# Two graph layers on one core: seven-product sets begun two columns earlier with their sums made in place, and block row 0 worked off in four stripes

## The chip, the cores and the metric

The kernel runs on one core of one Trainium2 chip. The metric is the device time in microseconds (us) of a whole execution; lower is better.

## The reference

Two residual graph layers over 8192 nodes with 64 features, all in float32. `adj` is a dense 8192 x 8192 array of 256 MiB that is used by both layers.

```python
def layer0(x, adj, u):                 # dropout on x, then the graph product
    keep = (u >= 0.1)
    return adj @ (x * keep / 0.9)
def layer1(x, adj, weight, bias):
    return adj @ (x @ weight) + bias
x = layernorm(x + layer0(x, adj, u))   # call it h
x = layernorm(x + layer1(x, adj, weight, bias))
```

## The kernel before

The adjacency is cut into 16 x 16 tiles of 512 x 512 numbers (1 MiB each), `adj_t[i, j]`, laid out on the host as [128, 4, 512]: four slices of 128 sources j by 512 outputs i. `stat` holds for each block j the dropped-out x (64 numbers) and, once it is known, h (64 numbers); they are the stationary operands, a tile is the moving one. TensorE writes 64 result rows at a time, so that products go in couples: one into the lower 64 PSUM partitions, one into the upper 64, side by side. One matmul of the program is two records of the trace.

Row i of h needs all 16 tiles of row i with x (layer 0). Column j of the second product needs h of block j. A tile (i, j) with j < i can serve both on one visit. A tile with j > i comes too early for h; it is kept on the chip when it is within HOLD = 3 of the diagonal, else loaded a second time (78 tiles, so 334 loads in all).

The function `order_of_work` writes out one list of jobs, which all engines follow:

- **first** (i, j): the tile with x, four matmuls of 512 columns (L731) into the two banks `sum_f`.
- **second** (L806) and **pair** (L800): one or two tiles with h into one of three `echo` banks; VectorE then adds the bank to `layer2` (`join`, L554 and L644).
- **both**: first and second on one tile. **early** (L784): two tiles of columns 0 to 3, rows 4 to 15, with x and with h in turn, two echo banks, added to `layer1` and `layer2`.
- **fused**, in rows above EARLY = 4 and columns 4 to 13: seven products on quarters of the tile instead of eight, 14 matmuls of 256 columns (L749 to L766). Four of its seven operand pairs are sums of quarters, which VectorE makes in `operands` (L581, L583, L584) in a buffer apart, `tile_sums`, up to AHEAD = 3 jobs ahead. The products of a row gather in two `products` banks; `combine` adds them up once per row.
- **row_end**, **turn**: ScalarE and VectorE copy the row's sum to `halves` (L447, L651, L655), TensorE transposes it (L824), VectorE and ScalarE make the layernorm (L668 to L676), and h of the block is ready. FILL = 6 half jobs stand after row_end to cover this chain.
- **final** (L839): the product with the weight, eight times at the end, then the second layernorm and the store.

The planner keeps a running `lead`: each job adds its TensorE time (WORK) and takes off 16 for each load; with the lead under LEAD it takes a heavy or early job, else a light one. In the inner loop at most MOST_IN_A_ROW = 2 heavy jobs follow each other while others are left. `place_tiles` gives each tile one of SLOTS = 16 slots of 8 KiB per partition; SyncE issues all loads in order (L392), each behind the tile job that frees its slot. x and u come in five groups through the last four slots (L370, L371), and VectorE drops out and reduces them (L528 to L544); the maximum of |x| gives the scale of h.

VectorE is in order: it walks the same list, doing the joins, the sums for fused jobs, the combine and the layernorm chain.

Of the kernel before, what the change touches and what calls it, by code (L numbers as in the profile page):

```python
# [30 lines left out]
P = 128  # L31
# [9 lines left out]
SLOTS = 16  # L41
EARLY = 4
HOMES = 5
AHEAD = 3
# [3 lines left out]
WORK = {"first": 11, "second": 11, "both": 22, "fused": 19, "pair": 22, "early": 44}  # L48
# [6 lines left out]
XU_GROUPS = ((4, 5), (5, 8), (8, 12), (12, 16), (0, 4))  # L55
XU_BEFORE = (1, 3, 6, 10)
# [18 lines left out]
TILE_JOBS = ("fused", "both", "first", "second", "pair", "early")  # L75
HALVES = {"first": 1, "second": 1, "both": 2, "fused": 2, "pair": 2, "early": 4}


def tiles_of(job):
    kind, i, j = job  # L80
    return [(i, j), (i + 1, j)] if kind in ("pair", "early") else [(i, j)]

# [14 lines left out]

def order_of_work():
# [6 lines left out]
    def put(job):  # L105
        nonlocal lead
        if job[0] in ("first", "both", "fused", "early"):
# [6 lines left out]
    for i in range(NB):  # L114
# [5 lines left out]
        if i >= 1:  # L120
            filler = []
            while sum(HALVES[job[0]] for job in filler) < FILL:
                choice = [early] if lead < LEAD and early else [again] if i > 7 else []
                choice = [jobs_of for jobs_of in (*choice, light, again, early, heavy, near) if jobs_of]
                filler.append(choice[0].pop(0))
                put(filler[-1])
                if len(filler) == 1:
                    jobs.append(("turn", i - 1))
            for job in seconds_of([r for r in range(NB) if held(r, i - 1)], i - 1):
                put(job)  # L130
            again += seconds_of([r for r in range(i - 1) if not held(r, i - 1)], i - 1)
            if i - 1 < EARLY:
                early = sorted(early + [("early", r, i - 1) for r in range(EARLY, NB, 2)], key=lambda job: job[1:])
# [40 lines left out]
    return jobs  # L174


def place_tiles(jobs):
# [7 lines left out]
    for m, job in enumerate(tile_jobs):  # L185
        for tile in tiles_of(job):
            if tile not in on_chip:
                on_chip[tile] = len(needs)
                needs.append([tile, m, []])
            needs[on_chip[tile]][2].append(m)  # L190
            if not (job[0] == "first" and held(*tile)):
                del on_chip[tile]

    free = [(0, s, 0) for s in range(SLOTS)]
    loads, place = [], {}
    for tile, begin, uses in needs:
        free.sort(key=lambda t: t[0])
        freed, slot, use = free.pop(0)
        assert freed <= begin, "the order of work needs more slots"
        loads.append((*tile, slot, use, freed, tile_jobs[begin][0]))  # L200
        free.append((uses[-1] + 1, slot, use + 1))
        for m in uses:
            place[tile_jobs[m], tile] = (slot, use)
# [3 lines left out]
def resnorm_graph_layers(nc: bass.Bass, x, adj_t, u, weight, bias, out):  # L207
# [15 lines left out]
    latest_freed, freed_for = 0, {}  # L223
    for load in loads:
        latest_freed = max(latest_freed, load[4])
        freed_for[load[0:2], load[5]] = latest_freed


    sums_from, chain_at = [], 0
    for job in jobs:  # L230
        if job[0] in ("row_end", "turn"):
            chain_at = done_after[job]
        elif job[0] == "fused":
            n = len(sums_from)
            begin = max(tile_jobs.index(job) - AHEAD, freed_for[job[1:3], "fused"], chain_at)
            if n >= 2:
                begin = max(begin, tile_jobs.index(fused_jobs[n - 2]) + 1)
            sums_from.append(begin)
    joined = [job for job in jobs for _ in range({"second": 1, "both": 1, "pair": 1, "early": 2}.get(job[0], 0))]
    finals = [job[1] for job in jobs if job[0] == "final"]  # L240

    complete = {i: max(n for n, job in enumerate(joined) if job[1] in (i, i + 1)) + 1 for i in range(0, NB, 2)}
# [7 lines left out]
    with ctx:  # L250
# [10 lines left out]
        tile_sums = sb("tile_sums", [P, 2, 4, 2, B // 2])  # L261
# [26 lines left out]
        def stat_sums(j):  # L288


            n = j - EARLY
            home = stat_homes[:, n] if n < HOMES else layer1[:, n - HOMES]
            return home.rearrange("p (v k f) -> p v k f", v=4, k=2)

# [31 lines left out]

        s_arrived = [sem(f"tile_arrived_{n}") for n in range(SLOTS)]
        s_xu = [sem(f"xu_loaded_{n}") for n in range(len(XU_GROUPS))]
# [8 lines left out]
        half_by_dve = sem("half_of_row_summed")  # L337
        operands_ready = sem("tile_sums_ready")
# [21 lines left out]

        row_0 = [job[2] for job in jobs if job[0] in TILE_JOBS][:NB]
        assert row_0 == sorted(row_0, key=lambda j: [a <= j < b for a, b in XU_GROUPS].index(True))

# [3 lines left out]
        def _(sp):  # L367
# [7 lines left out]
            for n, (i, j, slot, use, freed, kind) in enumerate(loads):  # L375
# [7 lines left out]
                if i == rows_begun and kind in ("first", "fused"):  # L383
                    if i >= 2:
                        sp.wait_ge(turned_read, i - 1)
                    sp.dma_start(x_res[:, i % 2], x_v[:, i]).then_inc(s_res[i % 2], 16)
                    rows_begun += 1
                if use == 0 and staged <= slot:
# [3 lines left out]
                sp.dma_start(tiles[:, slot], adj_t[i, j]).then_inc(s_arrived[slot], 16)  # L392
# [6 lines left out]
        def _(pool):  # L399
# [9 lines left out]
            pool.wait_ge(turned_read, NB)  # L409
            pool.wait_ge(turned_ready, NB)  # L410
            pool.wait_ge(h_ready, NB)
# [17 lines left out]
        def _(act):  # L429
# [10 lines left out]
            for job in jobs:  # L440
                if job[0] == "row_end":
                    i = job[1]
                    if i:
                        act.wait_ge(turned_ready, i)
# [3 lines left out]
                elif job[0] == "turn":  # L448
                    act.wait_ge(centred, job[1] + 1)
# [8 lines left out]
        def _(dve):  # L458
# [59 lines left out]
            def pair_inverse_root(n):  # L518
                if n >= 2:
                    dve.wait_ge(y_ready, n - 1)  # L520
                return inverse_root(rstd[:, n % 2], var[:, n % 2], root[:, n % 2], 2 * C, NB + n + 1)
# [35 lines left out]
            n_operands = 0  # L557
            n_combined = 0

            def sum_stat(j):  # L560

                dve.wait_ge(h_ready, j + 1)
# [10 lines left out]
            def operands(n):  # L573

                _, i, j = fused_jobs[n]
                if n >= 2:
                    dve.wait_ge(tile_jobs_done, done_after[fused_jobs[n - 2]])
                slot, use = place[fused_jobs[n], (i, j)]
                dve.wait_ge(s_arrived[slot], 16 * (use + 1))
                tile, a = tiles[:, slot], tile_sums[:, n % 2]  # L580
                step(dve.tensor_tensor(out=a[:, 0:2], in0=tile[:, 0:2].rearrange("p k (v m) -> p v k m", v=2),  # L581
                                       in1=tile[:, :, B // 2:B].rearrange("p (v k) m -> p v k m", v=2), op=ALU.add))
                step(dve.tensor_tensor(out=a[:, 2], in0=a[:, 1], in1=tile[:, 0:2, 0:B // 2], op=ALU.add))  # L583
                dve.tensor_tensor(out=a[:, 3], in0=tile[:, 2:4, 0:B // 2], in1=a[:, 2],  # L584
                                  op=ALU.add).then_inc(operands_ready, 1)

            def combine(i):
# [18 lines left out]
                step(plus(second[:, left], products[1][high, right]), 3)  # L606
# [261 lines left out]
```

## Time and profile before

| | us |
|---|---|
| median of 3 runs | 920.83 (919.95 to 921.16) |
| profiled execution, own time | 920.42 |
| profiled execution, span | 918.6 |
| TensorE matmul busy | 884.0 |
| VectorE busy | 448.6 |
| ScalarE, GpSimd busy | 28.7, 24.3 |
| DMA | 359.49 MB, mean 391 GB/s |

The span is what the profiler recorded from the first to the last instruction; 1.8 us of the execution's time lie outside it. "Busy" of TensorE counts the time in which at least one matmul is under way. A mean duration of a matmul includes its way through the array, so that two neighbours overlap; the pace is read from the starts.

### The profile page before, as it was taken

To read this page: it belongs to the slowest core of one execution; us is meant where nothing else is said; L and a number is where in the kernel's file an instruction comes from. 1 tells how busy PE (TensorE), PEld (TensorE's weight loads), DVE (VectorE), ACT (ScalarE), POOL (GpSimd) and SP (SyncE) were. 2 spreads that over 40 slices of the span, in tenths; PEclk is the share of its full clock that TensorE was granted. 3 is DMA by queue.
4 is the path that set the end of the run, shared out by engine and by line. 5 is a ranking of instruction groups with operands and counts; after the bars stand their busy time and mean duration, and the time that the engine had idled before them with its cause. 6 is when DMAs were issued, how large, how long until landed. Compare 5 with 4: busy or idle time off the path is not lost.

```text
span 918.6 us, 11872 instructions
## 1 busy us (share of the span) xinstructions
PE 884.0 (96%) x5070; PEld 363.0 (40%) x5070; DVE 448.6 (49%) x804; ACT 28.7 (3%) x66; POOL 24.3 (3%) x24
## 2 busy tenths in 40 slices
PE   4689999999999999999999999999999999999996
PEld 0123333333333333333444445354544635546342
DVE  4320122114113126155674767586768576777556
ACT  0010000000000000000000000000000000000011
POOL 3000000000000000000000000000000000000123
PEclk9899999999999999999999999999999999999998
DMA  9999999988997989999999999999999999999972
GB/s 350 400 421 421 421 420 422 421 360 352 422 375 281 422 330 376 421 420 416 417 376 420 421 410 418 383 425 383 414 385 411 420 420 421 420 421 420 421 327 69
DMA packets 57348, 359.49 MB, mean 391 GB/s; under 512 B 6352, under 2 KB 14544, under 8 KB 14544
## 3 DMA queue, kind: packets, MB, share of 16 engines
q1 hardware_dynamic: 57296, 358.74, 95.2%
q8 instruction: 40, 0.66, 0.3%
q14 instruction: 12, 0.10, 0.0%
HBM read 356.61 MB, written 2.10 MB: 390 GB/s over the span
## 4 chain that ended last, share of the span: by engine, by line
PE 91%; DMA 5%; SPq 3%; DVE 1%; issue 0%; ACT 0%; DVEq 0%
PE psum L731 23%; PE psum L800 22%; PE psum L784 18%; PE psum L749 6%; PE psum L759 6%; PE psum L764 6%; PE psum L806 5%; DMA tiles<-adj_t 5%; PE psum L754 3%; SPq L392 2%; PE psum L824 1%; PE psum L839 1%; SPq L371 1%; SPq L370 0%; PE psum L766 0%
## 5 line engine op out<-in xcount | busy, mean ns | idle before, releaser
L731 PE MATMUL psum<-tiles,stat 128*64 128x512 f32 x1144 | 263.8, 605 | 25.6 <-DMA tiles<-adj_t 25.5
L554 DVE TENSOR_TENSOR layer<-psum,layer 128x512 f32<-128x512 f32 (+1 forms) x132 | 91.0, 689 | 253.8 <-PE psum L784 160.7
L800 PE MATMUL psum<-tiles,stat 128*64 128x512 f32 x944 | 210.6, 594 | 0.0
L784 PE MATMUL psum<-tiles,stat 128*64 128x512 f32 x768 | 169.1, 593 | 0.4 <-issue 0.4
L731 PEld LDWEIGHTS psum<-tiles,stat 128*64 128x64 f32 x1144 | 81.5, 139 | 189.2 <-issue 143.9
L800 PEld LDWEIGHTS psum<-tiles,stat 128*64 128x64 f32 x944 | 66.5, 137 | 126.3 <-issue 124.9
L581 DVE TENSOR_TENSOR tile_sums<-tiles 128x1024 f32<-128x1024 f32 x65 | 79.5, 1223 | 42.5 <-PE psum L766 39.7
L784 PEld LDWEIGHTS psum<-tiles,stat 128*64 128x64 f32 x768 | 55.2, 137 | 108.3 <-issue 108.3
L751 PE MATMUL psum<-tiles,stat 128*64 128x256 f32 x260 | 66.7, 379 | 0.0
L749 PE MATMUL psum<-tiles,stat 128*64 128x256 f32 x260 | 66.7, 379 | 0.0
L766 PE MATMUL psum<-tile_sums,stat 128*64 128x256 f32 x260 | 66.7, 379 | 0.0
L749 PEld LDWEIGHTS psum<-tiles,stat 128*64 128x64 f32 x260 | 35.6, 137 | 29.0 <-issue 13.7
L806 PE MATMUL psum<-tiles,stat 128*64 128x512 f32 x200 | 47.0, 592 | 0.0
L764 PE MATMUL psum<-tiles,stat_homes 128*64 128x256 f32 x180 | 46.2, 379 | 0.0
L761 PE MATMUL psum<-tile_sums,stat_homes 128*64 128x256 f32 x180 | 46.2, 379 | 0.0
L759 PE MATMUL psum<-tile_sums,stat_homes 128*64 128x256 f32 x180 | 46.2, 379 | 0.0
L583 DVE TENSOR_TENSOR tile_sums<-tile_sums,tiles 128x512 f32<-128x512 f32 x65 | 45.0, 692 | 2.2
L584 DVE TENSOR_TENSOR tile_sums<-tiles,tile_sums 128x512 f32<-128x512 f32 x65 | 45.0, 692 | 2.2
L751 PEld LDWEIGHTS psum<-tiles,stat 128*64 128x64 f32 x260 | 35.6, 137 | 0.0
L766 PEld LDWEIGHTS psum<-tile_sums,stat 128*64 128x64 f32 x260 | 35.6, 137 | 0.0
L447 ACT ACTIVATE halves<-psum 64x512 f32<-64x512 f32 x16 | 9.5, 592 | 732.1 <-PE psum L731 732.1
L759 PEld LDWEIGHTS psum<-tile_sums,stat_homes 128*64 128x64 f32 x180 | 24.7, 137 | 13.0
(83 smaller groups left out, 542.1 us busy)
## 6 DMA issues: line engine op xcount, KB each, us to landing
tiles<-adj_t SPq DMA_DIRECT2D x334, 1024.0 KB, 12.8
x_res<-x SPq DMA_DIRECT2D x16, 128.0 KB, 12.1
out<-layer SPq DMA_DIRECT2D x8, 256.0 KB, 2.1
tiles<-u SPq DMA_DIRECT2D x3, 512.0 KB, 14.2
tiles<-x SPq DMA_DIRECT2D x3, 512.0 KB, 15.2
tiles<-u SPq DMA_DIRECT2D x1, 384.0 KB, 6.3
tiles<-x SPq DMA_DIRECT2D x1, 384.0 KB, 6.9
tiles<-u SPq DMA_DIRECT2D x1, 128.0 KB, 2.2
```

The costliest lines, as they stand in the source:

```text
L554: return dve.tensor_tensor(out=to, in0=addend, in1=to, op=ALU.add)
L581: step(dve.tensor_tensor(out=a[:, 0:2], in0=tile[:, 0:2].rearrange("p k (v m) -> p v k m", v=2), in1=tile[:, :, B // 2:B].rearrange("p (v ...
L731: last = pe.matmul(sum_f[i % 2][to, :], stat[:, j * C + c, 0:D], tile[:, c], start=begun.get("f") != i and c < 2, stop=ends and c >= 2, sk ...
L749: pe.matmul(products[0][low, left], stat[:, j * C + k, 0:D], tile[:, k, left], start=new and k == 0, stop=False, skip_group_check=True)
L751: pe.matmul(products[0][high, left], stat[:, j * C + 2 + k, 0:D], tile[:, 2 + k, left], start=new and k == 0, stop=False, skip_group_check ...
L759: pe.matmul(products[1][low, left], t[:, 2, k], a[:, 2, k], start=new and k == 0, stop=False, skip_group_check=True)
L761: pe.matmul(products[1][high, left], t[:, 0, k], a[:, 1, k], start=new and k == 0, stop=False, skip_group_check=True)
L764: pe.matmul(products[1][low, right], t[:, 3, k], tile[:, 2 + k, right], start=False, stop=False, skip_group_check=True)
L766: last = pe.matmul(products[1][high, right], stat[:, j * C + 2 + k, D:2 * D], a[:, 3, k], start=False, stop=False, skip_group_check=True)
L784: last = pe.matmul(bank[to, :], stat[:, j * C + c, half], tile[:, c], start=c == 0, stop=c == C - 1)
L800: last = pe.matmul(bank[to, :], stat[:, j * C + c, D:2 * D], tile[:, c], start=c == 0, stop=c == C - 1)
L806: last = pe.matmul(bank[to, :], stat[:, j * C + c, D:2 * D], moving[0][:, c], start=c < 2, stop=c >= 2)
```

## The change

- Fused jobs begin at column 2 and row 3 (EARLY = 2). The buffer `tile_sums` is gone. The sums are written over the tile itself by four VectorE instructions of 128x512. For this each fused job is cut in two: **raw** runs the six matmuls that need quarters as loaded (top left, bottom left, and bottom right), **fused** the eight that need sums. `with_raw` puts the raw job one tile job ahead of its fused job. The signs in `combine` and `stat_sums` homes follow.
- Block row 0 is worked off in four stripes of 128 outputs (**part** q, g: four tiles' stripes), each with its own row_end, transpose and layernorm (part_end, part_turn). The host lays out `adj_parts` (single stripes of tiles 0 to 3) and `adj_0` (stripes of four tiles, 1 MiB) for it.
- As soon as a quarter of h of block 0 is there, column 0 of rows 2 to 13 is worked off by **chunk** and **rest** jobs: one load of 1 MiB brings, from four rows, the slices that meet that quarter (`adj_chunks`); each job does two of the rows, with x and with h, two echo banks, two joins. They replace six of the early jobs (columns 0, rows 2 to 13).
- x and u come in the order of the blocks, all of them within the first stripe. SLOTS is 17, HOMES 6.

```diff
-SLOTS = 16
-EARLY = 4
-HOMES = 5
-AHEAD = 3
+SLOTS = 17
+EARLY = 2
+HOMES = (NB - 2 - EARLY) // 2
+KEPT_PIECES = 1
+PARTS = 4
-XU_GROUPS = ((4, 5), (5, 8), (8, 12), (12, 16), (0, 4))
-XU_BEFORE = (1, 3, 6, 10)
+XU_GROUPS = ((0, 1), (1, 4), (4, 8), (8, 12), (12, 16))
+XU_BEFORE = (1, 4, 5, 6)
...
+def with_raw(jobs):
+    out = []
+    for job in jobs:
+        if job[0] == "fused":
+            at = len(out)
+            while at > 1 and out[at - 1][0] not in TILE_JOBS:
+                at -= 1
+            out.insert(at - 1, ("raw", *job[1:]))
+        out.append(job)
+    return out
...
+    for q in range(PARTS):
+        for g in range(groups):
+            jobs.append(("part", q, g))
+            if q and g == 0:
+                jobs.append(("part_turn", q - 1))
+            elif chunks_due and (q > 1 or g > 1):
+                jobs += chunks_due[:2]
+                chunks_due = chunks_due[2:]
+            if g == 0 and q:
+                chunks_due += chunk_jobs(q - 1)
+        jobs.append(("part_end", q))
...
+            late = chunk_jobs(PARTS - 1)
+            early = [("early", r, 0) for r in range(rows_of_chunk((NB - EARLY) // PARTS - 1).stop, NB, 2)]
+            pieces += [late[n:n + 2] for n in range(0, len(late), 2)]
+            used = len(pieces) - KEPT_PIECES
...
-        tile_sums = sb("tile_sums", [P, 2, 4, 2, B // 2])
...
+            def second_sums(n):
...
+                dve.wait_ge(s_arrived[slot], 16 * load)
+                dve.tensor_tensor(out=tile[:, top, right], in0=tile[:, top, right], in1=tile[:, bottom, right],
+                                  op=ALU.add).then_inc(first_sums_ready, 1)
+                dve.wait_ge(first_sums_ready, n + 1)
+                dve.wait_ge(tile_jobs_done, done_after["raw", i, j])
+                dve.tensor_tensor(out=tile[:, top, left], in0=tile[:, top, left], in1=tile[:, top, right],
                                   op=ALU.add).then_inc(operands_ready, 1)
+                dve.wait_ge(operands_ready, 3 * n + 1)
+                dve.tensor_tensor(out=tile[:, bottom, left], in0=tile[:, bottom, left], in1=tile[:, top, left],
+                                  op=ALU.add).then_inc(operands_ready, 1)
+                dve.tensor_tensor(out=tile[:, bottom, right], in0=tile[:, top, left], in1=tile[:, bottom, right],
+                                  op=ALU.subtract).then_inc(operands_ready, 1)
...
+                if kind == "part":
...
+                    for k in range(PARTS):
...
+                        for c in range(C):
+                            to = slice(0, D) if c % 2 == 0 else slice(D, P)
+                            last = pe.matmul(sum_f[bank][to, 0:P], stat[:, j * C + c, 0:D], moving[:, c],
+                                             start=j == 0 and c < 2, stop=j == NB - 1 and c >= 2,
+                                             skip_group_check=True)
...
+                elif kind in ("chunk", "rest"):
...
+                    for half in slice(0, D), slice(D, 2 * D):
+                        if n_second >= ECHO_BANKS:
+                            pe.wait_ge(added, n_second - ECHO_BANKS + 1)
+                        bank = echo[n_second % ECHO_BANKS]
+                        n_second += 1
+                        pe.matmul(bank[0:D, :], stat[:, c, half], moving[:, n], start=True, stop=True)
+                        last = pe.matmul(bank[D:P, :], stat[:, c, half], moving[:, n + 1], start=True, stop=True)
...
+                        pe.wait_ge(operands_ready, 3 * n + 1)
                         for k in range(2):
...
+                            pe.matmul(products[1][low, left], t[:, 2, k], tile[:, k, left],
+                                      start=False, stop=False, skip_group_check=True)
+                            pe.matmul(products[1][high, left], t[:, 0, k], tile[:, k, right],
+                                      start=False, stop=False, skip_group_check=True)
+                        pe.wait_ge(operands_ready, 3 * n + 3)
...
```

## Rows read from the trace of the kernel before

**Rows 1.** The page: busy time by engine, and the chain that ended last.
```profile
PE 884.0 (96%) x5070; PEld 363.0 (40%) x5070; DVE 448.6 (49%) x804; ACT 28.7 (3%) x66; POOL 24.3 (3%) x24
PE 91%; DMA 5%; SPq 3%; DVE 1%; issue 0%; ACT 0%; DVEq 0%
```

**Rows 2.** Windows of 10 us: busy by engine, then PEclk, DMA share, GB/s.
```profile
10.00:20.00 10.00, 5.40 (x20) 0.97 (x16) 5.27 (x7) 0.00 (x0) 0.00 (x0) 1.00 1.04 399
40.00:50.00 10.00, 6.58 (x20) 1.83 (x18) 4.65 (x7) 0.00 (x0) 0.00 (x0) 0.66 1.01 413
70.00:80.00 10.00, 9.44 (x44) 3.15 (x46) 0.69 (x1) 0.00 (x0) 0.00 (x0) 1.00 1.01 420
200.00:220.00 20.00, 20.00 (x96) 6.79 (x94) 7.91 (x19) 0.71 (x3) 0.00 (x0) 1.00 0.69 274
```

**Rows 3.** TensorE's timeline, rows 0 and 1: start, us, line, count [idle before <-releaser].
```profile
31.02 7.23 PE L731 MATMUL psum<-tiles,stat 128*64 128x512 f32 x24 [3.54 <-DMA tiles<-adj_t]
70.02 1.94 PE L731 MATMUL psum<-tiles,stat 128*64 128x512 f32 x8 [0.55 <-DMA tiles<-adj_t]
72.50 1.94 PE L731 MATMUL psum<-tiles,stat 128*64 128x512 f32 x8 [0.54 <-DMA tiles<-adj_t]
74.27 3.60 PE L800 MATMUL psum<-tiles,stat 128*64 128x512 f32 x16
```

**Rows 4.** The chain of waits in order of time: start, us, what.
```profile
107.05 6.87 PE psum L784 x32
113.92 8.58 PE psum L731 x40
```

**Rows 5.** Groups of instructions: busy us, mean ns, idle before.
```profile
L731 PE MATMUL psum<-tiles,stat 128*64 128x512 f32 x1144 | 263.8, 605 | 25.6 <-DMA tiles<-adj_t 25.5
L749 PE MATMUL psum<-tiles,stat 128*64 128x256 f32 x260 | 66.7, 379 | 0.0
L581 DVE TENSOR_TENSOR tile_sums<-tiles 128x1024 f32<-128x1024 f32 x65 | 79.5, 1223 | 42.5 <-PE psum L766 39.7
L583 DVE TENSOR_TENSOR tile_sums<-tile_sums,tiles 128x512 f32<-128x512 f32 x65 | 45.0, 692 | 2.2
```

**Rows 6.** Timeline inside a fused job, TensorE, and VectorE's start behind it.
```profile
763.38 0.38 PE L766 MATMUL psum<-tile_sums,stat 128*64 128x256 f32 x1
763.60 0.38 PE L766 MATMUL psum<-tile_sums,stat 128*64 128x256 f32 x1
764.02 1.23 DVE L581 TENSOR_TENSOR tile_sums<-tiles 128x1024 f32<-128x1024 f32 x1 [0.34 <-PE psum L766]
```

**Rows 7.** VectorE's timeline: two sums of a fused job, then two joins.
```profile
351.87 0.69 DVE L583 TENSOR_TENSOR tile_sums<-tile_sums,tiles 128x512 f32<-128x512 f32 x1
352.59 0.69 DVE L584 TENSOR_TENSOR tile_sums<-tiles,tile_sums 128x512 f32<-128x512 f32 x1
353.31 0.69 DVE L554 TENSOR_TENSOR layer<-psum,layer 64x512 f32<-64x512 f32 x1
354.04 0.69 DVE L644 TENSOR_TENSOR layer<-psum,layer 64x512 f32<-64x512 f32 x1
```

**Rows 8.** Timeline of the last two final jobs on TensorE, 128 columns each.
```profile
907.91 1.93 PEld L839 LDWEIGHTS psum<-w,layer 64*128 64x128 f32 x32 [0.81 <-issue]
907.91 2.12 PE L839 MATMUL psum<-w,layer 64*128 64x128 f32 x32
```

**Rows 9.** Weight loads of 64 columns, all of L731.
```profile
L731 PEld LDWEIGHTS psum<-tiles,stat 128*64 128x64 f32 x1144 | 81.5, 139 | 189.2 <-issue 143.9
```

**Rows 10.** VectorE's work on a group of x and u, and the last reduction.
```profile
41.42 1.23 DVE L528 SCALAR_TENSOR_TENSOR stat<-tiles 128x1024 f32<-128x1024 f32 x1 [8.57 <-DMA tiles<-x]
45.79 0.22 DVE L539 TENSOR_REDUCE x_largest<-x_largest 128x1 f32<-128x5 f32 x2
```

**Rows 11.** The layernorm chain of row 0 on VectorE, first and last instruction.
```profile
63.09 0.42 DVE L668 TENSOR_TENSOR work<-psum,x_res 128x256 f32<-128x256 f32 x1
67.70 0.48 DVE L676 SCALAR_TENSOR_TENSOR stat<-work,h_scale,rstd 128x256 f32<-128x256 f32 x1
```

More of the change, by code:

```diff
@@ L47 @@
 ECHO_BANKS = 3
-WORK = {"first": 11, "second": 11, "both": 22, "fused": 19, "pair": 22, "early": 44}
+WORK = {"chunk": 11, "rest": 11, "first": 11, "second": 11, "both": 22, "fused": 19, "pair": 22, "early": 44}
 WORK_OF_LOAD = 16
@@ L72, in seconds_of, with rows_of_chunk, first_row, chunk_jobs @@
     return jobs
-TILE_JOBS = ("fused", "both", "first", "second", "pair", "early")
-HALVES = {"first": 1, "second": 1, "both": 2, "fused": 2, "pair": 2, "early": 4}
+TILE_JOBS = ("part", "chunk", "rest", "raw", "fused", "both", "first", "second", "pair", "early")
+HALVES = {"part": 1, "chunk": 1, "rest": 1, "first": 1, "second": 1, "both": 2, "fused": 2, "pair": 2, "early": 4}
 def tiles_of(job):
     kind, i, j = job
+    if kind == "part" and j == 0:
+        return [(0, k) for k in range(PARTS)]
+    if kind in ("part", "chunk", "rest"):
+        return [("chunk" if kind == "rest" else kind, i, j)]
     return [(i, j), (i + 1, j)] if kind in ("pair", "early") else [(i, j)]
+def rows_of_chunk(g):
+    return range(EARLY + PARTS * g, EARLY + PARTS * g + PARTS)
+def first_row(job):
+    return rows_of_chunk(job[1])[0 if job[0] == "chunk" else 2]
+def chunk_jobs(c):
+    return [(kind, g, c) for g in range((NB - EARLY) // PARTS) for kind in ("chunk", "rest")]
+def turns(i):
+    return i + PARTS
 def begins_at(i):
@@ L106, in put @@
         nonlocal lead
-        if job[0] in ("first", "both", "fused", "early"):
+        if job[0] == "rest":
+            n = 0
+        elif job[0] in ("first", "both", "fused", "early", "chunk"):
             n = len(tiles_of(job))
@@ L222, in resnorm_graph_layers @@
     tile_jobs = [job for job in jobs if job[0] in TILE_JOBS]
[L223 to L229, printed above, removed]
-    for job in jobs:
[L231 to L239, printed above, removed]
+    second_sums_from = [done_after["raw", *job[1:]] for job in fused_jobs]
+    joined = []
+    for job in jobs:
+        if job[0] in ("chunk", "rest"):
+            joined += [first_row(job)] * 2
+        else:
+            joined += [job[1]] * {"second": 1, "both": 1, "pair": 1, "early": 2}.get(job[0], 0)
     finals = [job[1] for job in jobs if job[0] == "final"]
-    complete = {i: max(n for n, job in enumerate(joined) if job[1] in (i, i + 1)) + 1 for i in range(0, NB, 2)}
+    complete = {i: max(n for n, row in enumerate(joined) if row in (i, i + 1)) + 1 for i in range(0, NB, 2)}
     x_v = x.rearrange("(b p c) d -> p b (c d)", p=P, c=C)
@@ L374, in _ @@
             rows_begun = 0
-            for n, (i, j, slot, use, freed, kind) in enumerate(loads):
+            for n, (tile, part, slot, freed, new, kind) in enumerate(loads):
                 if n in XU_BEFORE:
@@ L809, in _ @@
                     n_second += 1
-                elif kind == "row_end" and job[1] == 0:
+                elif kind == "part_end" and job[1] == 0:
                     pe.wait_ge(identity, 2)
```

358 lines of the change are left out of this document (221 added, 137 removed).

## The prediction, made before the result was known

> **What bounds the kernel now.** I read the page first: TensorE has matmuls under way for 884.0 of 918.6 us, and 91% of the chain that ended last is TensorE's, 5% a tile's DMA [rows 1]. So the end is set by TensorE's work plus the time it lost. Where it lost time stands in the windows: in 10 to 20 us it is busy 5.40 of 10 while the DMA moves 399 GB/s, at 70 to 80 it reaches 9.44, and from there it is full to the last product [rows 2]. In the start it takes a tile every 2.50 us, the DMA's pace, and needs less for it [rows 3]. From 200 to 220 us the DMA itself falls to 274 GB/s with TensorE full: there all slots are taken and TensorE is the bound [rows 2]. VectorE, 448.6 us busy, has slack on average.
>
> TensorE's paces: 32 records of an early job take 6.87 us, so a couple of 512 columns takes 0.429, five first jobs 8.58 [rows 4], one 1.717; a tile with x and h costs 3.43. The couples of 256 columns start 0.22 apart (763.38, 763.60) [rows 6], taken as half of 0.429; a fused job has 14 of them, 3.00 us. The mean of 379 ns [rows 5] includes the way through the array and is no pace.
>
> **How much was lost at the start.** Row 1 ends at 113.92 + 8.58 = 122.5 us [rows 4]. By the order of work TensorE has then done 32 first jobs (54.9), one pair (3.4) and four early jobs (27.5), 85.9 us of work: 36.6 lost. It was already lost at 72.5, where the 22nd tile starts [rows 3]: 21 jobs before it are 36.1 us of work. Behind 122.5 nothing is missing but breaks at transposes and finals, which stay.
>
> **The change, part by part.**
>
> *Products.* Fused tiles were i - 4 in rows 5 to 14 (55) and 10 in row 15: 65. With EARLY = 2 they are 1 to 12 in rows 3 to 14 (78) and 12 in row 15: I count 90 (the change's title says 91; one more is 0.4 us). Each saves 3.43 - 3.00 = 0.43 us: 25 x 0.43 = **-10.7 us**, on the path, since these rows are TensorE's. Two more combines are VectorE's, beside 6.9 us of first jobs near the diagonal.
>
> *Loads.* Still 256 + 78 = 334: stripes and chunks bring the same bytes in pieces of 1 MiB (the first stripe 256 KiB). At 2.49 us a tile (1,048,576 bytes at 421 GB/s; the starts in [rows 3] give 2.48 to 2.50) they take 832 us, as before. Behind row 1, 291 loads take 725 us and TensorE has 744 plus 22 of breaks and finals: the DMA does not set the end, but its slack shrinks by the 10.7. Row by row I get TensorE ahead of the balance by 8 us in row 2, behind by 4 in row 3 and 1 in row 4, then even and rising from row 7. The lead it enters with (below) covers that. Cost 0; if a few loads come late in rows 3 to 8, 1 to 3 us. The extra slot against the tile held one job longer between raw and fused: 0.
>
> *Start.* Two limits. First the DMA: up to the last first job of row 1 there are 43 tiles (32, and 11 of the 12 chunk loads; one piece is kept). The 22nd landed at 72.5, the 43rd can at 72.5 + 21 x 2.49 = 124.8, and row 1 ends at 126.5. The work done by then is 54.9 + 3.4 + 11 x 3.43 = 96.1: 30.4 lost. Second TensorE's own path. By 20 us some 6.8 MB had come at 279 and then 399 GB/s; x, u and the first stripe are 8.4 MB, which ends near 26. x's last group is dropped out 1.9 us after it lands and reduced after some 3 more (1.23, then up to 45.79 from 41.42) [rows 10]; the scale's product waits for that at part_end 0 and stands before stripe 1, a new wait of about 1 us: TensorE goes on at 28.3 with 6.9 done, 21.4 lost. Stripe 1 runs at the DMA's pace until the first chunk job (its h needs the layernorm chain, 4.6 us plus one instruction in [rows 11], for a quarter of the columns shorter), some 2.5 more lost; from there a stripe and its three chunk loads are 17.2 us of work for 17.4 us of DMA, and 0.9 goes on transposes: 24.8 lost at the end of row 0.
>
> To that come three things. (a) The 128-column couples: ideally 0.107, a quarter of 0.429. Nearest row: 16 couples of 128 columns in 1.93 us of weight loads, 2.12 in all, 0.121 apart [rows 8]; those load 128 columns of weights, these 64. Lower end 0.107 (nothing), upper end 0.139, if the weight load of 139 ns [rows 9] could not hide. I take 0.121: 64 couples a stripe, the three later stripes pay 192 x 0.0135 = 2.6; in the first the DMA hides it. (b) The clock. From 40 to 50 us the granted clock is 0.66 [rows 2], that is, part of it at 1.2 GHz: it fell after idle gaps of 3.5 us like the one before 31.02 [rows 3]. The first stripe has such gaps too; before, the DMA hid most of the loss, now the time behind 36 us is dense. 0 to 5, I take 2. (c) Echo banks: a chunk job makes two joins of 0.73 [rows 7] in 1.72 us, and the chain of each part_turn holds them up for some 3.3 us, against three banks (2.6) and a stripe job (1.7) of cover: 0 to 3, I take 1. In all 30.4, and row 1's transpose makes 31. Both limits together, since neither is smooth: 31.5 lost, with 30.4 and 38 as ends. Against 36.6: **-5.1 us**.
>
> *Sums in place.* Before, a set was made ahead, in another buffer; TensorE never waited. Now a set is four instructions of 128x512, 0.692 each [rows 5], starts 0.72 apart [rows 7]: 2.90 us instead of 2.65, and three of them can begin only when the raw job is through. VectorE starts 0.21 after TensorE's pace has ended (763.60 + 0.215 to 764.02) [rows 6], so the last sum is there 0.21 + 2.17 = 2.38 us after raw, if VectorE is free. The second half of the fused job comes after the job between (1.72 at least) and its first half (0.86): 2.58. It fits by 0.2. In a long run of fused jobs raw and fused alternate, a set has 3.0 us for 2.90: it just fits too. Where it does not: a second job ("X") between, with two joins of 0.73, and exactly two fused jobs behind it. VectorE then does: first set until 2.4, the two joins until 3.8, the first sum of the second set until 4.6, and the rest until 6.7. TensorE would want to be at the second half of the second fused job at 1.72 + 1.29 + 1.72 + 0.86 = 5.6. Loss 1.2, and 0.15 more where a join stands before the raw job. With the old planner's order and EARLY = 2 this pattern stands at the head of rows 9, 11, 13, 15 (the held second (i-1, i-1)) and once in row 14. Five times 1.3 is 6.5, and small misses elsewhere 1. Ends: 0 (every set hidden, as now) and 0.3 for each of 90, 27. I take **+7.5 us**, nearer to the rows' own arithmetic than to either end. Behind the waiting sums stand the joins and the layernorm chain, but echo banks and FILL cover these.
>
> *Tail.* Finals and the last chain are untouched: 0.
>
> **The skill against it.** The couples of 128 columns in [rows 8] come 0.121 us apart, 0.06 a record. The Trainium skill ("TensorE: Matmul & The Clock Gate", section "Back-to-back issue gap") gives about 81 ns for a sustained matmul of 128 columns with its weight load, against the plain quotient of columns and clock. By that figure, as an estimate, the 512 records of row 0 would take 41.5 us instead of 27.4, and the three later stripes would put some 10.6 us on the path instead of 2.6. The row speaks against it, as products of 64 rows and two column halves run side by side, but not with this form.
>
> **Sum.** -10.7 - 5.1 + 7.5 = -8.3; span 918.6 - 8.3 = 910.3; 1.8 us lie outside the span, 912.1. The profiled execution (920.42) is 0.4 under the median of the runs: **912.5 us**.
>
> **Rivals.**
>
> *B, all sums hidden and the start at the DMA's limit*: -10.7 - 6.2 = -16.9, **904**. For it: VectorE is idle for 39.7 us before the 65 first sums [rows 5], and the planner's order may differ from the one I used. Against: the arithmetic of the waits above.
>
> *C, stripes at the weight load's pace*: 0.139 for a couple, the later stripes pay 6.1 instead of 2.6: **916**. For it: the matmul of 128 columns is shorter than the 139 ns of [rows 9]. Against: [rows 8], where loads of 128 columns kept 0.121. By the page's 81 ns it would be 920.5.
>
> *D, slower: VectorE becomes the pace of the rows with products.* The set has 2.90 us in a period of 3.00. In place, each instruction reads and writes the tile that TensorE reads, on top of the DMA's writes; were it 0.79 instead of 0.725, a set would be 3.15 and 90 sets would each hold TensorE for 0.15, with the late ends on top: +13.5 to the forecast, **926**. It decides from 0.77 an instruction (3.09), where 90 x 0.09 eats the gain of 8.3. Against: every 512-column instruction of VectorE has 0.69, from PSUM, from the tile or mixed [rows 5, 7].
>
> *E, the change does not do what it says*: slots run short with the tile held from raw to fused, the DMA falls back in rows 3 to 8, and some 8 us come back as waits for tiles: **920**.
>
> **Chances.** Forecast 0.50, B 0.22, C 0.10, D 0.14, E 0.04. This kernel's runs tell about 0.2% (1.8 us) from no change: under 919.0 is faster, over 922.7 slower. Faster: nearly all of the forecast, B, most of C: 0.77. Same: E, bits of the others: 0.08. Slower: D and a little of the forecast's tail: 0.15. Range 901 to 922: below it 0.06 (B with a better start), above it 0.13 (D). The forecast's own range is 908 to 918, from 0.107 or 0.139 for the couples and 3 to 12 us of waits.
>
> **What would show it.** Row 1 ending near 127.6 (DMA's limit 126.5, before 122.5) with 11 chunk loads done: the start right. Couples of 128 columns 0.107, 0.121 or 0.139 apart: point (a), C. TensorE idle behind VectorE's last sum only at the heads of rows 9, 11, 13, 15 and in row 14, 1.2 to 1.4 each: the sums right; none: B; at nearly every fused job 0.1 or more, or VectorE's instructions of 0.75 and up: D. TensorE waiting for tiles behind row 1: E. My forecast is wrong if the starting loss is not between 30 and 38, or if waits behind row 1 are outside 3 to 12 us in all.

## The result, and the profile after

| | before | after |
|---|---|---|
| median, us | 920.8 (919.95 to 921.16, 4 runs) | 910.3 (910.11 to 910.64, 4 runs) |
| ratio | | 0.9891, 95% interval 0.9879 to 0.9904 |
| profiled span, us | 918.6 | 908.6 |
| VectorE busy, us | 448.6 | 540.9 |

The changed kernel is 1.1% faster, by an interval that is clear of no change; 912.5 had been forecast. First the page of the changed kernel, the lines that answer to [rows 1]: busy time by engine, and the chain's shares.

```profile
PE 877.6 (97%) x5754; PEld 410.9 (45%) x5754; DVE 540.9 (60%) x1043; ACT 30.4 (3%) x75; POOL 25.1 (3%) x24
PE 90%; DMA 4%; DVE 2%; SPq 1%; issue 1%; ACT 0%; DVEq 0%
```

VectorE's share of the chain goes from 1% to 2%, the DMA's from 5% to 4%. Its groups, and the stripes' matmuls, against [rows 5]:

```profile
L682 DVE TENSOR_TENSOR tiles<-tiles 128x512 f32<-128x512 f32 x90 | 62.3, 692 | 40.3 <-PE psum L915 38.1
L687 DVE TENSOR_TENSOR tiles<-tiles 128x512 f32<-128x512 f32 x90 | 61.6, 684 | 0.0
L869 PE MATMUL psum<-tiles,stat 128*64 128x128 f32 x512 | 36.8, 305 | 17.6 <-DMA tiles<-adj 9.5
```

There are 90 sets, as the prediction counted, and an instruction in place takes what one into another buffer took (0.692 us [rows 5]). The start, as in [rows 3]: TensorE's timeline of row 1 (start, us, line, count, idle before), and VectorE's first instruction behind the row's end.

```profile
113.66 1.94 PE L924 MATMUL psum<-tiles,stat 128*64 128x512 f32 x8 [0.20 <-DMA tiles<-adj_t]
116.15 1.94 PE L924 MATMUL psum<-tiles,stat 128*64 128x512 f32 x8 [0.56 <-DMA tiles<-adj_t]
117.92 3.60 PE L971 MATMUL psum<-tiles,stat 128*64 128x512 f32 x16
121.35 7.04 PE L924 MATMUL psum<-tiles,stat 128*64 128x512 f32 x32
128.51 0.69 DVE L783 COPY halves<-psum 64x512 f32<-64x512 f32 x1 [6.25 <-PE psum L924]
```

The last two first jobs ahead of the pair start 2.49 apart and wait for their tiles, as in the kernel before. Then come a pair and four first jobs whose tiles are there, and row 1 ends at 128.4 (the copy starts 0.1 later), with 96.1 us of work done: 32.3 lost, where it was 36.6. From 38.3 us, where the chunk jobs begin, to the end of row 1 TensorE waits for the DMA three times (0.52 at 106.21 and the two above, of 0.20 and 0.56), 1.3 us in all.

The windows that answer to [rows 2] (busy by engine, then PEclk, DMA share, GB/s):

```profile
0.00:10.00 10.00, 1.90 (x16) 1.53 (x18) 4.23 (x8) 1.28 (x1) 7.90 (x9) 1.00 0.80 256
10.00:20.00 10.00, 5.47 (x52) 4.66 (x48) 6.88 (x8) 0.00 (x0) 0.00 (x0) 0.83 1.06 388
20.00:30.00 10.00, 5.00 (x60) 4.76 (x62) 7.22 (x10) 0.00 (x0) 0.00 (x0) 0.79 1.06 392
```

In 10 to 20 us the DMA brings 388 GB/s where it was 399. And the waits of TensorE for other engines, in the whole trace (us in total, times, longest):

```profile
PE psum L933 <- DVE tiles L682: 0.9, 5, 0.2
PE psum L939 <- DVE tiles L687: 0.8, 5, 0.2
PE psum L924 <- DMA tiles<-adj_t: 0.8, 2, 0.6
```

Five places at which it waits for sums. This is the first one, the head of row 9: TensorE's single second job, its last matmul of the first fused job, VectorE from the joins of the single second job on, and the second fused job's two halves.

```profile
459.43 1.89 PE L977 MATMUL psum<-tiles,stat 128*64 128x512 f32 x8
461.65 0.67 DVE L650 TENSOR_TENSOR layer<-psum,layer 64x512 f32<-64x512 f32 x1
462.36 0.69 DVE L777 TENSOR_TENSOR layer<-psum,layer 64x512 f32<-64x512 f32 x1
462.98 0.68 DVE L678 TENSOR_TENSOR tiles<-tiles 128x512 f32<-128x512 f32 x1
463.69 0.69 DVE L682 TENSOR_TENSOR tiles<-tiles 128x512 f32<-128x512 f32 x1
463.95 0.38 PE L941 MATMUL psum<-tiles,stat 128*64 128x256 f32 x1
464.41 0.69 DVE L685 TENSOR_TENSOR tiles<-tiles 128x512 f32<-128x512 f32 x1
464.53 0.40 PE L933 MATMUL psum<-tiles,layer 128*64 128x256 f32 x1 [0.19 <-DVE tiles L682]
465.02 0.68 DVE L687 TENSOR_TENSOR tiles<-tiles 128x512 f32<-128x512 f32 x1
465.20 0.38 PE L933 MATMUL psum<-tiles,layer 128*64 128x256 f32 x1
465.76 0.43 PE L939 MATMUL psum<-tiles,layer 128*64 128x256 f32 x1 [0.15 <-DVE tiles L687]
```

The idle time in brackets is not the loss: a matmul is counted until it has left the array. The loss is read from the starts. Behind 463.95 the next was due at 464.17 and comes at 464.53, 0.36 late; behind 465.20 it was due at 465.42 and comes at 465.76, 0.34 late. 0.7 us at each place, 3.5 in all. The others (near 564, 675, 746 and 802 us) show the same two bracketed numbers: rows 11, 13, 14 and 15. In the order of work a single second job stands between two raw jobs in rows 7 and 12 too. There a third raw job stands between the two fused jobs, and TensorE does not wait.

### The profile page after: what moved, and what is told of

It is laid out like the page before. It is cut to its first block, busy times and chain, and to the rows that moved or that the text cites. A ratio compares the mean times of both kernels' runs of the same rounds, so it can differ in the third digit from the quotient of the medians.

```text
span 908.6 us, 13717 instructions
## 1 busy us (share of the span) xinstructions
PE 877.6 (97%) x5754; PEld 410.9 (45%) x5754; DVE 540.9 (60%) x1043; ACT 30.4 (3%) x75; POOL 25.1 (3%) x24
## 4 chain that ended last, share of the span: by engine, by line
PE 90%; DMA 4%; DVE 2%; SPq 1%; issue 1%; ACT 0%; DVEq 0%
PE psum L971 22%; PE psum L924 21%; PE psum L906 8%; PE psum L939 8%; PE psum L933 7%; PE psum L957 6%; PE psum L892 4%; PE psum L913 4%; PE psum L977 4%; DMA tiles<-adj_chunks 3%; PE psum L869 2%; DMA tiles<-adj 1%; PE psum L992 1%; PE psum L1007 1%; SPq L481 1%
## 5 line engine op out<-in xcount | busy, mean ns | idle before, releaser
L650 DVE TENSOR_TENSOR layer<-psum,layer 128x512 f32<-128x512 f32 (+1 forms) x143 | 98.6, 690 | 202.0 <-PE psum L971 102.9
L924 PE MATMUL psum<-tiles,stat 128*64 128x512 f32 x976 | 216.9, 593 | 0.8 <-DMA tiles<-adj_t 0.8
L971 PE MATMUL psum<-tiles,stat 128*64 128x512 f32 x944 | 211.7, 594 | 0.0
L924 PEld LDWEIGHTS psum<-tiles,stat 128*64 128x64 f32 x976 | 71.0, 137 | 128.2 <-issue 120.4
L971 PEld LDWEIGHTS psum<-tiles,stat 128*64 128x64 f32 x944 | 66.7, 137 | 123.5 <-issue 121.2
L941 PE MATMUL psum<-tiles,stat 128*64 128x256 f32 x360 | 92.7, 380 | 0.0
L906 PE MATMUL psum<-tiles,stat 128*64 128x256 f32 x360 | 92.4, 379 | 0.0
L908 PE MATMUL psum<-tiles,stat 128*64 128x256 f32 x360 | 92.4, 379 | 0.0
L682 DVE TENSOR_TENSOR tiles<-tiles 128x512 f32<-128x512 f32 x90 | 62.3, 692 | 40.3 <-PE psum L915 38.1
L906 PEld LDWEIGHTS psum<-tiles,stat 128*64 128x64 f32 x360 | 49.3, 137 | 40.9 <-issue 20.0
L685 DVE TENSOR_TENSOR tiles<-tiles 128x512 f32<-128x512 f32 x90 | 62.3, 692 | 3.1
L678 DVE TENSOR_TENSOR tiles<-tiles 128x512 f32<-128x512 f32 x90 | 61.9, 688 | 2.0
L687 DVE TENSOR_TENSOR tiles<-tiles 128x512 f32<-128x512 f32 x90 | 61.6, 684 | 0.0
L957 PE MATMUL psum<-tiles,stat 128*64 128x512 f32 x256 | 56.5, 593 | 0.6 <-issue 0.6
L869 PE MATMUL psum<-tiles,stat 128*64 128x128 f32 x512 | 36.8, 305 | 17.6 <-DMA tiles<-adj 9.5
L939 PE MATMUL psum<-tiles,stat_homes 128*64 128x256 f32 x192 | 49.3, 379 | 0.0
L908 PEld LDWEIGHTS psum<-tiles,stat 128*64 128x64 f32 x360 | 49.3, 137 | 0.0
L935 PE MATMUL psum<-tiles,stat_homes 128*64 128x256 f32 x192 | 49.3, 379 | 0.0
L933 PE MATMUL psum<-tiles,stat_homes 128*64 128x256 f32 x192 | 49.3, 379 | 0.0
L941 PEld LDWEIGHTS psum<-tiles,stat 128*64 128x64 f32 x360 | 48.8, 137 | 0.0
L892 PE MATMUL psum<-tiles,stat 128*64 128x512 f32 x96 | 45.2, 600 | 1.3 <-DMA tiles<-adj_chunks 0.7
L893 PE MATMUL psum<-tiles,stat 128*64 128x512 f32 x96 | 45.2, 601 | 0.0
```

The lines of the kernel that those rows point to most:

```text
L650: return dve.tensor_tensor(out=to, in0=addend, in1=to, op=ALU.add)
L682: dve.tensor_tensor(out=tile[:, top, left], in0=tile[:, top, left], in1=tile[:, top, right], op=ALU.add).then_inc(operands_ready, 1)
L685: dve.tensor_tensor(out=tile[:, bottom, left], in0=tile[:, bottom, left], in1=tile[:, top, left], op=ALU.add).then_inc(operands_ready, 1)
L892: pe.matmul(bank[0:D, :], stat[:, c, half], moving[:, n], start=True, stop=True)
L906: pe.matmul(products[0][low, left], stat[:, j * C + k, 0:D], tile[:, k, left], start=new and k == 0, stop=False, skip_group_check=True)
L908: pe.matmul(products[0][high, left], stat[:, j * C + 2 + k, 0:D], tile[:, 2 + k, left], start=new and k == 0, stop=False, skip_group_check ...
```

## The experiments

Every kernel below is the changed one with the edit shown, except the third. Times are medians; each was run beside the kernel before on the same chip (920.3 to 920.7 there). Differences to the changed kernel are taken from the medians; taken from the ratios they are at most 0.6 us different.

**The held single ahead of the held pair (e1).**

```diff
-        for job in seconds_of([r for r in range(NB) if held(r, i - 1)], i - 1):
+        for job in sorted(seconds_of([r for r in range(NB) if held(r, i - 1)], i - 1), key=lambda job: job[0] == "pair"):
```

> Only the order of the held second jobs differs: at the head of each row the single second job stands before the held pairs, so that the job between raw and fused at the heads of rows 9, 11, 13 and 15 is a pair (3.43 us) with one join instead of a single (1.72) with two. Theory (TensorE waits for VectorE's sums exactly where a single with two joins stands between raw and two fused jobs, 0.7 us each by the trace of the changed kernel, at five places): four of the five waits go, row 14 keeps its own; span 908.6 - 2.8 = 905.8, time 907.5. Rival (those waits are hidden by others, or the order is neutral): 910.3 as the changed kernel.

Measured 907.25, ratio 0.9857 (0.9844 to 0.9871), span 905.3. Its waits of TensorE for sums:

```profile
PE psum L933 <- DVE tiles L682: 0.2, 1, 0.2
```

Four of the five are gone, row 14 keeps its own, and 3.1 us went with them (2.8 expected). The rival, that the order is neutral, is out.

**65 sets instead of 90 (e2).**

```diff
-    return i > EARLY
+    return i > 4
...
-    return ("fused" if has_fused(i) and j < NB - 2 else "both", i, j)
+    return ("fused" if has_fused(i) and 4 <= j < NB - 2 else "both", i, j)
```

> Columns 2 and 3 of rows 3 to 15 by both jobs (eight products), as fused jobs only from column 4 and row 5: 65 sets instead of 90; stripes, chunks and sums in place stay. Theory: 25 x 0.43 = 10.7 us of TensorE's work come back, four of the five waits at row heads go with them (the two both jobs stand between), -2.8: time 910.3 + 7.9 = 918.2. Rival (the 25 sets bring less because waits for VectorE or for tiles take their place): under 914. This kernel is also the stripes alone against the kernel before: theory 920.8 - 4.3 for the start and +0.7 to 1.5 for waits.

Measured 919.78, ratio 0.9995 (0.9986 to 1.0004): 9.5 us over the changed kernel instead of 7.9. The gain of the 25 sets is there, but the four waits that I took off had successors, in TensorE's timeline at 349, 390, 427 (a wait for the last sum only, 0.15 in brackets) and 755 us; the last is this:

```profile
755.30 0.40 PE L933 MATMUL psum<-tiles,layer 128*64 128x256 f32 x1 [0.99 <-DVE tiles L682]
756.54 0.43 PE L939 MATMUL psum<-tiles,layer 128*64 128x256 f32 x1 [0.15 <-DVE tiles L687]
```

A both job has the same two joins as a single, and stands ahead of or behind a raw job in rows 6 to 8; in row 14 one stands ahead and a single between, and the wait is 0.8 us longer (0.99 in brackets for 0.19). So stripes and in-place sums, without the further products, are worth nothing that can be told from no change: the start's gain of 4.9 us (row 1 ends at 127.8 with the same 96.1 of work) is used up by such waits and by what else is lost behind row 1.

**The products without the stripes (e3).** The kernel before with this and the code that goes with it (row 0 in whole tiles, column 0 by early jobs):

```diff
-SLOTS = 16
-EARLY = 4
+SLOTS = 17
+EARLY = 2
...
+            out.insert(at - 1, ("raw", *job[1:]))
```

> The kernel before with only the products part: columns 2 and 3 by fused jobs (90 sets), raw jobs, sums in place, 17 slots; row 0 as before, in whole tiles, and column 0 by early jobs. Theory: the two parts add up; -10.7 for the products, +3.5 for waits at the five row heads and 0.5 for others: 920.8 - 6.7 = 914.1. Rival (the products need the start's lead of tiles, without it the DMA falls short in rows 3 to 8): 917 or more, with waits of TensorE for tiles behind row 1. Rival (the start is worth nothing): 910.3.

Measured 913.95, ratio 0.9931 (0.9919 to 0.9944), 6.3 us under the kernel before. The start is the old one (the 22nd tile, before at 72.50):

```profile
72.74 1.94 PE L760 MATMUL psum<-tiles,stat 128*64 128x512 f32 x8 [0.55 <-DMA tiles<-adj_t]
```

It has the same five waits and none for tiles behind row 1, so the rival is out: the products do not need the stripes' start. The stripes bring the other 3.7 us on top.

**Two sums of four (e4).**

```diff
-                dve.tensor_tensor(out=tile[:, bottom, left], in0=tile[:, bottom, left], in1=tile[:, top, left],
-                                  op=ALU.add).then_inc(operands_ready, 1)
-                dve.tensor_tensor(out=tile[:, bottom, right], in0=tile[:, top, left], in1=tile[:, bottom, right],
-                                  op=ALU.subtract).then_inc(operands_ready, 1)
```

> The third and fourth sum of each set are left out, so that two fused operands are not the right ones (this part of the computation is wrong); everything else as in the changed kernel. Theory: TensorE never waits for VectorE any more, all of the 0.7 us at each of five row heads goes: span 905.1, time 906.8. Rival (VectorE's load of 541 us slows more than these five places, through the pace in long runs or contention for the tiles): 903 or less.

Measured 906.63, ratio 0.985 (0.9837 to 0.9864). With VectorE at 425.3 us instead of 540.9, 3.7 us go and no more, and no wait for sums is left: the 115.6 us of VectorE's work that were left out had cost the five waits and little else. Two sums in place remain, so what these cost by contention for the tiles is not shown.

**The last chunk load ahead of row 1's end (e7).**

```diff
-KEPT_PIECES = 1
+KEPT_PIECES = 0
```

> KEPT_PIECES 0: the last chunk load of column 0 is worked off in row 1 instead of behind its end; the work in all is the same. Theory (the start is set by the DMA at one point, the job first (1, 15), which began at 116.15 us with 84.1 us of work done, 32.1 lost): a chunk load has 3.43 us of work for 2.49 of DMA, so one more of them ahead of that point takes 0.9 off the loss: row 1's end at 130.9 instead of 128.2 with 3.4 more work done, time 909.4. Rival (TensorE's own path or its clock in the start sets it): 910.3, unchanged.

Measured 914.63, ratio 0.994 (0.9927 to 0.9952): 4.3 us slower, where I expected 0.9 faster. TensorE's timeline at row 1's end:

```profile
129.58 1.94 PE L924 MATMUL psum<-tiles,stat 128*64 128x512 f32 x8 [0.97 <-DMA tiles<-adj_t]
134.62 7.09 PE L957 MATMUL psum<-tiles,stat 128*64 128x512 f32 x32 [3.10 <-issue]
147.78 3.65 PE L971 MATMUL psum<-tiles,stat 128*64 128x512 f32 x16 [1.91 <-DVE stat L739]
```

I had looked at one point where the DMA binds. The next is behind it: the first filler is now an early job, which needs two further tiles, 5 us of DMA, and begins 3.1 us after the row's last matmuls had ended; the transpose stands behind it, so h comes late too, and TensorE waits 1.9 for it. The view names no releaser for the 3.10. That it is these two tiles follows from the DMA's pace: a tile each 2.49 us from first (1, 15) on, which began at 116.15 as the 39th, gives the 46th at 133.6. In the changed kernel the same job begins at 133.62, 0.64 late and behind the kept piece and the transpose, so that moving the piece does not let it begin earlier; in e7's profile it begins 1.0 later still. My choice of the point was wrong. The piece that is kept is the work that covers these tiles.

**A warm TensorE in the first stripe (e6).**

```diff
+                    if q == 0 and g:
+                        if g == 1:
+                            pe.wait_ge(identity, 2)
+                        for _ in range(DUMMIES):
+                            pe.matmul(echo[0][:, 0:P], ident[:, :], ident[:, :], start=True, stop=True)
```

> Ten products of the identity with itself, into an echo bank that nobody reads yet, stand ahead of each of the stripe jobs (0,1), (0,2) and (0,3), to fill TensorE's gaps in the first stripe. Theory (DMA's limit at first (1, 15)): whatever the granted clock does between 10 and 34 us (0.83, 0.79 and 0.87 in the windows of the changed kernel), row 1 ends where it did, time within 0.5 of 910.3. Rival (the low clock in the start costs on the path): the clock is 1.0 there and 2 to 3 us go, 907.7.

Measured 910.4, ratio 0.9893 (0.988 to 0.9907), the same as the changed kernel. The window, to be held against the one above (0.83):

```profile
10.00:20.00 10.00, 9.99 (x91) 9.30 (x90) 6.47 (x7) 0.00 (x0) 0.00 (x0) 1.00 1.06 389
```

The granted clock is 1.00, that is 2.4 GHz, there and from 20 to 40 us, and it gives nothing: the low clock of the start is hidden behind the DMA. One point was not as expected: in the profiled execution, at 911.3 the longest of the four, row 1 ends 1.0 later than in the changed kernel's (129.4). The other three lie between 910.2 and 910.5.

**Both orders at once (e8).** The first edit and KEPT_PIECES = 0.

> KEPT_PIECES 0 and the single second jobs ahead of the pairs at the row heads, both. Theory: the gains add up, -3.1 as measured for the order of the held jobs and -0.9 for the piece: 906.3. Rival (the piece gives nothing): 907.3.

Measured 909.91, ratio 0.9889 (0.9876 to 0.9903): worse than the first alone by 2.7, not by the 4.3 that the piece cost in the kernel as it is. The expected 906.3 took a gain for the piece that e7 had not. In the two profiled executions, 4.4 us apart where e1 and the changed kernel are 3.3 apart, the early job behind row 1 begins at 133.54 here and at 134.62 in e7, 1.1 earlier, which accounts for that difference. Why it did, and the other 0.6 of the 1.7 between the medians, stays open.

**A fifth VectorE instruction in each set (e5).**

```diff
+                dve.wait_ge(operands_ready, 4 * n + 3)
+                dve.tensor_tensor(out=tile[:, bottom, right], in0=tile[:, top, left], in1=tile[:, bottom, right],
+                                  op=ALU.subtract).then_inc(operands_ready, 1)
```

> The fourth sum of each set is made twice (its value is then not the right one), one more VectorE instruction of 0.7 us per fused job, 63 us in all. Theory (a set of 2.7 us only just fits the 3.00 us of a fused job, VectorE has no more to give there): with 3.4 a set VectorE is the pace of the long runs, and the last sum comes 0.4 late at the single ones; 90 x 0.4 = 36, and more at the heads: 943 to 952. Rival (VectorE, busy 60% of the span, has slack to take it): under 920.

Measured 955.9, ratio 1.038 (1.0364 to 1.0396): 45.6 us more, 0.51 per set, a little over the range. TensorE's waits:

```profile
PE psum L942 <- DVE tiles L690: 24.6, 50, 0.9
PE psum L936 <- DVE tiles L682: 8.5, 14, 0.9
```

VectorE is busy 63% of that span, and TensorE waits for it at 64 places. From one set to the next, in a long run of fused jobs:

```profile
480.00 0.69 DVE L682 TENSOR_TENSOR tiles<-tiles 128x512 f32<-128x512 f32 x1 [1.83 <-PE psum L918]
483.51 0.69 DVE L682 TENSOR_TENSOR tiles<-tiles 128x512 f32<-128x512 f32 x1
```

A set of five takes 3.51 us, 0.51 more than the 3.00 of a fused job, which is the loss per set. So the edge is one instruction away: it lies between the 2.76 us of a set of four (below) and 3.51, and that it is at 3.00, as D has it, fits this loss.

**The joins behind the sums, TensorE's order untouched (e9).**

```diff
+                if put_off is not None and job[0] != "raw":
+                    join_single(put_off)
+                    put_off = None
+                if job[0] == "second" and jobs[at - 1][0] == "raw" and jobs[at + 1][0] == "raw":
+                    put_off = job
+                    continue
```

> TensorE's order is that of the changed kernel. Only VectorE's changes: where a single second job stands between two raw jobs, its two joins are made behind the next set of sums instead of ahead of it. Theory (the five waits come from these two joins, 1.4 us, standing ahead of the second set): all five go, TensorE waits for no sums any more, as in the kernel with two sums: span 905, time 906.8 (910.3 - 3.5). Rival (the order e1 won by the longer job between, or by something else in its order, not by the joins): 909 or more.

Measured 906.34, ratio 0.9844 (0.9831 to 0.9857). VectorE at the head of row 9, second set and then the joins:

```profile
461.71 0.69 DVE L678 TENSOR_TENSOR tiles<-tiles 128x512 f32<-128x512 f32 x1
462.67 0.69 DVE L682 TENSOR_TENSOR tiles<-tiles 128x512 f32<-128x512 f32 x1 [0.27 <-PE psum L930]
464.01 0.68 DVE L687 TENSOR_TENSOR tiles<-tiles 128x512 f32<-128x512 f32 x1
464.61 0.68 DVE L650 TENSOR_TENSOR layer<-psum,layer 64x512 f32<-64x512 f32 x1
```

The last sum starts at 464.01, 1.0 earlier; no wait for sums is left in the trace. With nothing changed in TensorE's order this pins the cause: two joins ahead of the second set. 4.0 us went where the waits were 3.5; the profiled execution reaches row 1's end 0.3 earlier, which the edit does not touch.

**Both cures (e10).**

> The singles ahead of the pairs at the row heads, and the joins of the one single left between two raw jobs (row 14) behind the sums. Theory: the one wait that e1 kept, 0.7, goes, and nothing else is left to win: 906.6, the same as the kernel with two sums. Rival (the two changes take the same gain from different places and add up): 904.

Measured 906.18, ratio 0.9843 (0.9829 to 0.9856), within the runs of the one before it: they cure the same thing. It is the fastest version of those that leave nothing out, 4.1 us under the changed kernel.

**Without u (e11).**

```diff
-                sp.dma_start(u_stage[:, b], u_v[:, b]).then_inc(s_xu[g], 16)
...
-                    out=stat[:, t, 0:D], in0=u_stage[:, b].rearrange("p b (c d) -> p (b c) d", d=D), scalar=DROP,
+                    out=stat[:, t, 0:D], in0=x_stage[:, b].rearrange("p b (c d) -> p (b c) d", d=D), scalar=DROP,
```

> u is not loaded, and x stands in its place in the comparison, so that the dropout is not the right one; 2.1 MB less come in the first 25 us, TensorE's work is the same. Theory (the start is the DMA's to the end of row 1): 2.1 MB at 421 GB/s are 5.0 us, and all of it comes out at the end: 905.3. Rival (TensorE's own path in rows 0 and 1 is as long as the DMA's): at most 2 us, 908.3 or more.

Measured 904.16, ratio 0.9821 (0.9807 to 0.9834): 6.1 us less for 2.1 MB. The row ends here:

```profile
122.03 0.69 DVE L782 COPY halves<-psum 64x512 f32<-64x512 f32 x1 [6.24 <-PE psum L923]
```

6.5 earlier. The start is the DMA's. Of the 1.1 us over 5.0 the slower DMA of the first 30 us explains 0.4 (2.1 MB at some 390 GB/s are 5.4), the rest stays open.

## Why the prediction was right, point by point

- **Products, -10.7.** 90 sets, as counted. e3 with the five waits on it gives -6.3: -10.7 + 3.5 = -7.2, and 0.9 are left over, 0.2 of them in the start (row 1's end at 122.7 for 122.5), the rest not traced. The other way round, e2 gives back 9.5 for 25 sets less, with four waits in place of five. Right, as far as runs that change other things too can show it.
- **Start, -5.1.** Measured 36.6 - 32.3 = **-4.3**. The DMA's limit was the right mechanism (nothing from the clock in e6, 6.1 us from fewer bytes in e11) and 1.3 us too early: first (1, 15), the 39th load in whole tiles, was due at 72.5 + 17 x 2.49 = 114.8 and began at 116.15. The DMA moves 256 GB/s in the first 10 us and 388 and 392 in the next two windows, less than the 279 and 399 that I took from the kernel before. Over the first 70 us it has moved 0.4 MB less, an estimated 0.9 us at 421 GB/s. TensorE went on with stripe 1 at 31.1, not at 28.3. The job that waited last was this one, not row 1's last, whose tile was there in time. TensorE's own path was nearly as long, since it waits only 1.3 us for the DMA behind 38.3; the forecast had the two 0.6 apart (30.4 and 31 lost). Of the three additions, (a) was too dear: 32 couples of a stripe take 3.71 us with their 0.18 at the end, 0.110 apart, 0.003 over the ideal, so that the three later stripes pay 0.6 us and not 2.6:

```profile
34.01 3.71 PE L869 MATMUL psum<-tiles,stat 128*64 128x128 f32 x64
```

  (b) The clock fell as feared (0.83, 0.79) and cost nothing in e6. (c) A chunk load loses 0.11 at an echo bank (a couple at 46.33 instead of 46.22) and takes 3.59 us (43.65 to 47.24) for 3.43; over the 11 loads that is an estimated 1.8, for the 1 that I took. Rival C is out. The Trainium skill's 81 ns for a sustained matmul of 128 columns ("TensorE: Matmul & The Clock Gate", section "Back-to-back issue gap") was no guide for this form, couples of two column halves: 0.055 us a record here.
- **Sums in place, +7.5.** The mechanism and all five places were right, the size of a wait was half. Behind row 1 the changed kernel takes 908.6 - 128.4 = 780.2 for 744.3 us of work, 35.9 over; the kernel before 796.1 for 765.2, 30.9 over. **+5.0**, of which 3.5 are the five waits and 1.5 are left without VectorE's waits as well (e4: 904.6 - 127.8 = 776.8, 32.5 over). Of these, 0.45 lie right behind row 1: TensorE waits 0.20 for the kept piece's tiles and 0.64 ahead of the early job, where it waited 0.39 in the kernel before. The rest was not traced.

  (The 22 us of breaks and finals in the prediction's sum of loads are 30.9 by these numbers. That leaves the DMA more room and changes nothing in the sum.)

  I took 1.3 for a wait, it is 0.7. The mis-sized term is VectorE's step: I took 0.72 to 0.73 from start to start for every pair of instructions from [rows 7]. In the changed kernel's sets the last sum waits for nothing of the one before and starts 0.60 to 0.62 behind it in all 90 sets (464.41 to 465.02); so does a set's first sum behind a join (462.36 to 462.98, 0.62). Where an instruction waits for the one before it is 0.71 to 0.73. A set is 2.76 us and not 2.90, the joins 1.33 and not 1.45. The second set's last sum releases TensorE 6.33 us behind the end of the first raw job (459.43 to 465.76), where I had 6.7: that is 0.4 of the 0.6 by which I had a wait too long. The rest is the 0.15 that I had added for a join ahead of the raw job: its 0.07 is within the 6.33.

  The wait is not the whole condition: in [rows 7] L554 waits for nothing of L584 and starts 0.72 behind it (352.59 to 353.31). Of the 20 such pairs that the timeline of the kernel before lists one by one, 7 are 0.60 or 0.61 apart and 13 are 0.72 or more; what decides it stays open.

  The Trainium skill ("VectorE: DVE Perf Modes", section "The DRAIN you can't avoid") says that a semaphore after each instruction costs nothing extra. Each of these instructions releases one, those that are followed at 0.61 too, so the trace agrees for the release; where the next instruction waits for it, the trace has 0.1 us more.
- **Rivals.** B's upper half, sums all hidden, was false as the kernel stands and true with the joins moved (906.3). D was false, but only just: one more instruction per set brings 45.6 us. An instruction takes 0.69 in place as before. E: TensorE waits 0.8 us for whole tiles of adj_t in the whole run, all of it in row 1, besides the 0.84 right behind it.

The sum: -4.3 - 10.7 + 5.0 = -10.0, the spans' difference. The errors of start and sums (0.8 less and 2.5 more gain) partly cancel, and that the total comes out 2.2 us from the forecast is in part luck.

## What to carry to other kernels

An engine that walks one list in order can be late at a few places with 40% of its time free; look for the places where its own longer jobs stand ahead of what another engine waits for, and move those behind. It cost nothing on the other engine here, and it brought 4.0 us, as much as the restaged start. The place to look for is a pair of sets needed one right behind the other: where a further raw job stood between, the same two joins cost nothing. Where the start is the DMA's, add up loads and work to each job that waits, not to one: the point that binds moves on when the one before it is eased.

## What the runs showed of the hardware

- VectorE on 128x512 float32, in the changed kernel's sets: 0.61 us from start to start without a wait between two instructions, 0.71 to 0.73 with one. In place or into another buffer, 0.69 us each.
- Couples of 128-column matmuls with 64-column weights run at 0.110 us, though each weight load takes 0.14.
- 2.1 MB less to load at the start are 6.1 us at the end of a kernel that is TensorE's for its last 780 us.
